# A local-attention feed-forward stage, layer by layer, is rewritten as four passes of one layer and one sequence each

## The reference, cut to what matters

```
x = x + 0.5 * L0_ffn(layernorm(x))       # local attention and GEGLU, 2 layers
x = x + L0_attn(layernorm(x))            # attention with relative positions
x = x + 0.5 * L0_ffn(layernorm(x))
x = x + 0.5 * L1_ffn(layernorm(x))       # top 8 of 64 experts, plus a shared one
x = x + L1_attn(layernorm(x))            # state space model
x = x + 0.5 * L1_ffn(layernorm(x))

def _layer(x, wqkv, qs, ksc, wo, lg, lb, w1, b1, w2, b2):   # inside L0_ffn
    h = shift_token(x)                       # second half of the features one token later
    q, k, v = split(h @ wqkv, 3)             # 8 heads of 64
    q, k = l2norm(q) * qs, l2norm(k) * ksc
    q, k = rotary_xpos(q, k)
    o = local_attention(q, k, v)             # each token sees itself and the 64 before it
    x = x + o @ wo
    h = layernorm(shift_token(x)) * lg + lb
    a, g = split(h @ w1 + b1, 2)             # 341 each
    return x + (a * gelu(g)) @ w2 + b2
```

## Time and profile before

| | us |
|---|---|
| median of 3 runs (5562.16 to 5575.62) | 5565.12 |
| the profiled execution, its own time | 5573.75 |
| its span | 5572.0 |
| a feed-forward stage with experts, from its norm to its end | 231.3 |
| the two layers of a feed-forward stage alone | 240.6 |
| an attention stage with the state space model (its two ends read off the trace) | 164 |

### The profile page before, as it was taken

How to read it: one execution, slowest core, us unless ns; L and a number is a source line. 1 busy time by engine, 2 the same in 40 slices (tenths; PEclk the granted TensorE clock), 3 DMA queues, 4 the chain that set the end, 5 groups by cost and what they waited for, 6 DMA issues and landing times. The chain is left out here.

```text
span 5572.0 us, 51193 instructions
## 1 busy us (share of the span) xinstructions
PE 4237.3 (76%) x16034; PEld 2320.4 (42%) x16034; DVE 3172.3 (57%) x5382; ACT 2506.1 (45%) x5663; POOL 1501.4 (27%) x1096
## 2 busy tenths in 40 slices
PE   5686688787876878777886878768787787877756
PEld 3444444444533544344444434434443444444312
DVE  3323365765556555755557655575556655575576
ACT  2343344543454434634446444554346444464332
POOL 2102131531125112421215322251114312252111
PEclk7787798998998989989899889989899898999877
DMA  3020011210121110311103111121112111031122
GB/s 89 1 76 0 2 47 39 83 52 28 48 65 59 44 36 31 105 35 33 43 20 106 45 31 47 59 67 48 31 36 96 40 33 44 23 106 43 37 70 69
DMA packets 188817, 273.95 MB, mean 49 GB/s; under 512 B 23448, under 2 KB 102900, under 8 KB 188532
## 3 DMA queue, kind: packets, MB, share of 16 engines
q1 hardware_dynamic: 167652, 234.89, 13.4%
q10 hardware_dynamic: 20880, 35.52, 2.1%
HBM read 215.54 MB, written 54.79 MB: 49 GB/s over the span
## 5 line engine op out<-in xcount | busy, mean ns | idle before, releaser
L638 DVE SCALAR_TENSOR_TENSOR psum<-work,psum 128x512 f32<-128x512 f32 x528 | 366.6, 694 | 600.5 <-ACT work L576 599.4
L1463 POOL MEMSET work<- 128x256 f32 x32 | 10.0, 311 | 2323.8 <-POOLq L1265 1165.4
L1426 ACT ACTIVATE work<-psum,work 128x128 f32<-128x128 f32 (+1 forms) x1024 | 389.8, 393 | 421.6 <-DVE work L1523 421.4
L553 PE MATMUL psum<-work,w_up 128*128 128x512 f32 x1024 | 572.7, 643 | 1.5 <-DVE work L632 1.5
L558 PE MATMUL psum<-work,w_down 128*128 128x512 f32 x1024 | 551.9, 621 | 20.4 <-DVE work L645 18.2
L576 ACT ACTIVATE work<-psum 128x512 f32<-128x512 f32 x528 | 317.4, 601 | 345.2 <-PE psum L553 276.3
L1288 PE MATMUL psum<-ident,work 128*128 128x128 f32 x1024 | 187.1, 343 | 330.7 <-POOL work L1477 330.6
L1344 PE MATMUL psum<-work 128*128 128x64 f32 x3072 | 415.8, 291 | 0.0
L1344 PEld LDWEIGHTS psum<-work 128*128 128x128 f32 x3072 | 388.1, 204 | 39.0 <-issue 32.2
L1470 POOL TENSOR_TENSOR work<-work,minus_half 128x16 f32<-128x16 f32 x128 | 374.3, 2924 | 10.7
L645 DVE TENSOR_TENSOR work<-work,psum 128x512 f32<-128x512 f32 x512 | 351.4, 686 | 19.6 <-DMA work<-expert_weight_rows 2.1
(11 more groups left out here) (210 smaller groups left out, 8834.6 us busy)
## 6 DMA issues: line engine op xcount, KB each, us to landing
work<-expert_weight_rows SPq DMA_DIRECT2D x1024, 128.0 KB, 2.9
position_scores<-work SPq DMA_DIRECT2D x64, 768.0 KB, 3.5
work<-position_scores SPq DMA_DIRECT2D x64, 512.0 KB, 3.8
work<-state_readout_rows ACTq DMA_DIRECT2D x72, 256.0 KB, 3.4
cent<-state_readout_rows ACTq DMA_DIRECT2D x32, 256.0 KB, 3.6
sq<-state_readout_rows ACTq DMA_DIRECT2D x24, 256.0 KB, 3.6
rows<-in_L_attn_q SPq DMA_DIRECT2D x8, 256.0 KB, 3.7
expert_weight_rows<-work SPq DMA_DIRECT2D x16, 128.0 KB, 2.3
```

The costliest lines, as they stand in the source:

```text
L553: nc.tensor.matmul(UP, b.w_up[:, p * 128:(p + 1) * 128], self.xn, start=True, stop=True).then_inc(self.up, 1)
L638: v.scalar_tensor_tensor(out=UP, in0=self.tanh_h[p % self.turns][0:rows], scalar=1.0, in1=UP, op0=ALU.add, op1=ALU.mult).then_inc(self.sil ...
L1426: ins = s.activation(prob_of(u)[:, i, first:first + n], score_banks[:, i, first:first + n], ACT.Exp, bias=neg_max[:, t, 4 * half + i:4 * h ...
```

## The change

The two layers become four passes: pass i is layer i // 2 of sequence i % 2, with 256 tokens. Each pass is cut in steps: 5 of projection (P), 8 of attention (A) and 7 of mixing, norm and gated product (M). They run in one block, in seven phases: P of pass 0; A of 0 beside P of 1; A of 1 beside M of 0; M of 1 beside P of 2; A of 2 beside P of 3; A of 3 beside M of 2; M of 3. A step k of every engine's program holds the attention step, then the projection or mixing step, then the expert steps due. Those are dealt out as 3, 5, 5, 7, 5, 5 and 8, with 2 in the norm block (step 2, the top 8, moves from there to the first phase).

PSUM is dealt anew: scores have banks 0 and 1, turned weights bank 2 alone (six groups of four turned blocks in a pass, copied by ACT and DVE in turn), values bank 3, projection banks 4 and 5 (one product in each, evicted one by one), mixing 4 and 5 or 0 and 1, so that the experts keep only bank 6 for their up products beside bank 7 for the sum. The products behind the attention have 256 columns instead of 512. Where the experts run alone (the last round) they have three banks as before.

```diff
--- before.py
+++ after.py
...
-    BESIDE = ((5, 6), 7)
+    BESIDE = ((6,), 7)
...
-        self.aff = bank(b, self.ups[1])[:, 0:TILES * EXPERTS].rearrange("p (t e) -> p t e", t=TILES)
-        self.norm_banks = self.ups[0:2]
+        self.aff = bank(b, self.sum_bank)[:, 0:TILES * EXPERTS].rearrange("p (t e) -> p t e", t=TILES)
+        self.norm_banks = (self.ups[0], self.sum_bank)
...
-            beside.tensor(pe, upto=3)
...
-    for l in range(DEPTH):
-        ffn_layer(nc, b, prefixed(f"layer{l}"), l, beside, space, transfers if l == 0 else ([], None))
+    LocalFfn(nc, b, prefixed("passes"), space).run(beside, transfers)
...
+    PASSES = DEPTH * GROUP_SEQS
+    PROJECT, ATTEND, MIX = 5, 8, 7
...
+    @staticmethod
+    def where(i):
+        return i // GROUP_SEQS, slice(i % GROUP_SEQS * SEQ, (i % GROUP_SEQS + 1) * SEQ)
...
+    def mix_banks(i):
+        return (4, 5) if i % 2 == 0 else (0, 1)
...
+    def project_tensor(self, pe, i, k):
+        nc, b = self.nc, self.b
+        l, cols = self.where(i)
+        if k == 0:
+            pe.wait_ge(self.rows_shifted, i + 1)
+        for n in (2 * k, 2 * k + 1):
+            out = bank(b, 4 + n % 2)
+            if 10 * i + n >= 2:
+                pe.wait_ge(self.evicted, 10 * i + n - 1)
+            if k < 3:
+                t, part = n // 3, n % 3
+                at = cols.start + t * 128
+                nc.tensor.matmul(out, b.xn[:, at:at + 128], b.wqkv[:, l, part * INNER:(part + 1) * INNER],
+                                 start=True, stop=True).then_inc(self.projected, 1)
+            else:
+                t, part = k - 3, n % 2
+                if part == 0:
+                    pe.wait_ge(self.rotated, 2 * i + t + 1)
+                for j in range(4):
+                    at = part * INNER + j * 128
+                    ins = nc.tensor.transpose(out[:, j * 128:(j + 1) * 128], self.cosine[t][:, at:at + 128], b.ident[:])
+                ins.then_inc(self.projected, 1)
+
+    def project_scalar(self, act, i, k):
...
+    def project_vector(self, dve, i, t):
+        v, b = self.nc.vector, self.b
+        l, tile = i // GROUP_SEQS, 2 * i + t
+        dve.wait_ge(self.squared, tile + 1)
+        if i >= 1:
+            dve.wait_ge(self.rotated, tile - 1)
+            dve.wait_ge(self.projected, 10 * (i - 1) + 8 + 2 * t)
+        v.tensor_reduce(self.lens[t], self.sine[t].rearrange("p (h d) -> p h d", d=LD), AX, ALU.add).then_inc(self.summed, 1)
+        dve.wait_ge(self.summed, tile + 1)
+        for k in (1, 0):
+            r8, c8, s8 = (x[t][:, k * INNER:(k + 1) * INNER].rearrange("p (h d) -> p h d", d=LD) for x in (self.raw, self.cosine, self.sine))
+            table = lambda n, x0, x1: b.rope_w[:, l, n, t, x0:x1].unsqueeze(1).broadcast_to([128, LH, x1 - x0])
+            v.tensor_tensor(c8, r8, table(2 * k, 0, LD), ALU.mult)
+            v.tensor_tensor(s8[:, :, 0:32], r8[:, :, 32:64], table(2 * k + 1, 0, 32), ALU.mult)
+            ins = v.tensor_tensor(s8[:, :, 32:64], r8[:, :, 0:32], table(2 * k + 1, 32, 64), ALU.mult)
+            ins.then_inc(self.split if k == 0 else self.k_split, 1)
+        dve.wait_ge(self.k_split, tile + 1)
+        keys = slice(INNER, 2 * INNER)
+        v.tensor_tensor(self.cosine[t][:, keys], self.cosine[t][:, keys], self.sine[t][:, keys], ALU.add).then_inc(self.k_added, 1)
+
...
+    def turn_probs(self, pe, i, m):
+        nc, b = self.nc, self.b
+        u = self.UNIT_OF[m]
+        pe.wait_ge(self.exped, 4 * i + u + 1)
+        self.group_copied(pe, i, m - 1)
+        for n in range(4):
+            x, c = (n, 1) if u < 2 else (2 * (m % 2) + n // 2, n % 2)
+            ins = nc.tensor.transpose(bank(b, 2)[:, n * 128:(n + 1) * 128], self.probs[u % 2][:, x, c * 128:(c + 1) * 128], b.ident[:])
+        ins.then_inc(self.p_turned, 1)
+
...
+    def attend_tensor(self, pe, i, k):
+        if k == 0:
+            self.unit_scores(pe, i, 0)
+        elif k <= self.GROUPS:
+            m = k - 1
+            self.turn_probs(pe, i, m)
+            u = self.UNIT_OF[m]
+            if m in (0, 1, 2):
+                self.unit_scores(pe, i, u + 1)
+            if m >= 1:
+                self.values(pe, i, m - 1)
+        else:
...
+    def attend_scalar(self, act, i, k):
+        if k == 0:
+            if i == 0:
+                act.wait_ge(self.zeroed, 1)
+            self.exps(act, i, 0)
+        elif k <= self.GROUPS:
+            m = k - 1
+            if m % 2 == 0:
+                self.copy_probs(act, self.nc.scalar.copy, i, m, self.p_copied_a)
+            if m in (0, 1, 2):
+                self.exps(act, i, self.UNIT_OF[m] + 1)
...
+    def attend_vector(self, dve, i, k):
+        if k == 0:
+            self.maxima(dve, i, 0)
+        elif k <= self.GROUPS:
+            m = k - 1
+            if m in (0, 1, 2):
+                self.maxima(dve, i, self.UNIT_OF[m] + 1)
+            if m % 2 == 1:
+                self.copy_probs(dve, self.nc.vector.tensor_copy, i, m, self.p_copied_v)
+            if m == 2:
+                self.scale_heads(dve, i, 0)
+        else:
...
+    def run(self, beside, transfers):
+        P, A, M = self.PROJECT, self.ATTEND, self.MIX
+        due = lambda guests, k, n: (k + 1) * guests // n - k * guests // n
+
+        with self.nc.Block() as block:
+            @block.tensor
+            def _(pe):
+                for k in range(P):
+                    self.project_tensor(pe, 0, k)
+                    if k >= 2:
+                        beside.tensor(pe)
+                for k in range(A):
+                    self.attend_tensor(pe, 0, k)
+                    if k < P:
+                        self.project_tensor(pe, 1, k)
+                    beside.tensor(pe, due(5, k, A))
+                for k in range(A):
+                    self.attend_tensor(pe, 1, k)
+                    if k < M:
+                        self.mix_tensor(pe, 0, k)
+                    beside.tensor(pe, due(5, k, A))
+                for k in range(M):
+                    if k < P:
+                        self.project_tensor(pe, 2, k)
+                    self.mix_tensor(pe, 1, k)
+                    beside.tensor(pe, due(7, k, M))
+                for k in range(A):
+                    self.attend_tensor(pe, 2, k)
+                    if k < P:
+                        self.project_tensor(pe, 3, k)
+                    beside.tensor(pe, due(5, k, A))
+                for k in range(A):
+                    self.attend_tensor(pe, 3, k)
+                    if k < M:
+                        self.mix_tensor(pe, 2, k)
+                    beside.tensor(pe, due(5, k, A))
+                for k in range(M):
+                    self.mix_tensor(pe, 3, k)
+                    beside.tensor(pe, due(8, k, M))
...
+                for i in range(GROUP_SEQS):
+                    self.shift(dve, self.where(i)[1]).then_inc(self.rows_shifted, 1)
+                for k in range(P):
+                    if k in (1, 3):
+                        self.project_vector(dve, 0, k // 2)
+                    if k >= 2:
+                        beside.vector(dve)
+                for k in range(A):
+                    self.attend_vector(dve, 0, k)
+                    if k in (1, 3):
+                        self.project_vector(dve, 1, k // 2)
...
```

634 lines of the change are left out of this document (312 added, 322 removed).

## The result

| | before | after |
|---|---|---|
| median, us | 5570.17 (4 runs) | 5665.93 (4 runs, 5664.88 to 5670.4) |
| span of the profiled execution | 5572.0 | 5668.5 |
| a steady feed-forward stage, from its norm on | 231.3 | 244.8 |
| two layers of the two stages alone | 240.5 and 240.6 | 191.8 and 200.3 |

The ratio is 1.0175, with a 95% interval of 1.0157 to 1.0192. The change is slower by 96 us. The forecast was slower by 72, at 5637 us, with a range of 5480 to 5760.

The account below looks back on a forecast made before the run. Projection phases were taken as bound by a chain through four engines, attention with experts by TensorE. Fourteen stages at +8.5 us (+119) and the stages alone at -47 gave +72 on 5565: 5637 us, range 5480 to 5760.

Parts of the forecast that it names:

- tile 1's chain: A pass's second projected tile: DVE sums, POOL's power, addition and scaling, then TensorE turns it, 7.85 us after DVE starts.
- half clock: TensorE's slow clock behind a large gap ahead of the second tile's turning: 2.5 us charged in each of three phases.
- A steady stage: One of fourteen feed-forward stages with experts: the laid-out phases sum to 239.8 us against 231.3, +8.5.
- P alone: First phase, projection of pass 0 with no attention or mixing beside it: 23 us, second tile ready at 20.9.
- M beside P: Mixing of pass 1 beside projection of pass 2: 26.6 us of TensorE, waits 5.8 and 2.0, clock 2.5, total 36.9 us.
- The stages alone: The two stages at the start without experts: 217 us against 240.6 each, -47 us for both, bounds 200 to 235.
- The gap of 2.16 us: TensorE waits for step 2's exponentials in A beside P, the row maximum standing behind DVE's tile and expert: 1.7 us.
- Rival (a): Packing wins: laid-out waits overlap and the clock stays full; a stage 219 us, the kernel 5343 us; chance 0.12.
- Rival (b): Draw to small gain: laid-out waits right, no half clock; +1 us a stage, 5532 us (5480 to 5560); chance 0.25.
- Rival (c): Single expert bank decides: +23 us a stage, 5952 us, or likelier 5 or 6 us a stage, 5715; chance 0.13.
- Rival (d): A drain comes with table loads ahead of exponentials and gelu, as the skill page says: 133 us more, 5770; chance 0.02.
- table loads: ACT's loads rise from 9 to 16 a stage, 9.1 us; only 1.3 and part of the norm's wait on the path.

Follow-up runs that it names:

- Experiments 3: Changed kernel with the turning of a pass's second projected tile one step later on TensorE and ScalarE: 5512.61 us, ratio 0.9904.
- 8: Changed kernel with the expert put ahead of the second tile's turning in the fifth step beside a projection, on TensorE and ScalarE: 5522.86 us, ratio 0.9914.
- experiment 12: Experiment 11's order on VectorE, but with the second tile's turning one step later in place of one expert's step later: 5425.94 us, ratio 0.9739.
- experiment 4: Changed kernel with four idle products of 0.86 us on TensorE ahead of the wait for the second tile: 5601.55 us, ratio 1.0057.
- experiment 2: Kernel before, with the experts beside a stage given only bank 6 for up products instead of banks 5 and 6: 5576.72 us, ratio 1.0007.
- Experiment 5: Changed kernel with an exponential and a tanh in place of the passes' logarithm and gelu, leaving out 13 of 16 table loads a stage: 5603.88 us, ratio 1.0072.
- experiment 11: Experiment 10's kernel, with the second step's expert moved behind the third step's row maximum on VectorE in A beside P: 5461.3 us, ratio 0.9796.
- experiment 10: Kernel of 8, with VectorE's fourth-step tile piece opened between keys and queries for the expert's (beside mixing, the norm's) two operations: 5587.9 us, ratio 1.0023.

## Why the prediction was right, and where it wasn't

- **The side and the mechanism** were right: a stage is bound in its projection phases by tile 1's chain through DVE and POOL, and the change adds stretches in which TensorE must wait in order for it. Experiments 3 and 8 move that one wait, by a step or by one expert, and take 153 and 143 us. The place of the half clock was right in two of the three phases only: in the first A beside P it stands ahead of tile 1's gap and not behind it, so that 38.6 predicted against 38.8 measured is in part luck.
- **A steady stage: +8.5 predicted, +13.5 measured.** The mis-sized terms are P alone (23, measured 26.0), M beside P (36.9, measured 39.5) and the norm (8, measured 9.1), 6.7 us together; the others were within 1.7 us, and sum to 1.7 us less than predicted. In P alone DVE decides. The top 8, laid out at 2.5 us (10.6 to 13.1), takes 4.16 (2657.02 to 2661.18), since its last operation is five times as long as in the kernel before. So tile 1's sum starts at 15.0 and not at 13.1, its chain to the turning takes 8.42 us and not 7.8, and 2.6 us and not 2.1 are left behind it, at half clock: 3.0 us in all. The clock of 0.63 in the window is little of it, since TensorE is idle for 11.75 us ahead of the two turnings. In M beside P I had charged 2.5 us for the clock, in one stretch; there are two, behind the gap in the norm's chain and behind tile 1's. The charge was worked out of half-clock stretches of 3.4 to 6.8 us, of which the rows of before show the 6.8 alone. These errors of 5.0 us a stage were multiplied by fourteen: +70 us.
- **The stages alone: -47 predicted, -89 measured.** 217 us was to be compared with 191.8 and 200.3. The terms that failed are the attention phases, A beside M above all. I had 36 us for each A beside M, without a layout, and they take 30.1 and 27.1 in the first stage (clock 0.89 and 1.00) and 30.8 and 30.6 in the second (0.82 twice). A beside P, taken near its half-clock value (37 and 37.5), takes 33.0 and 31.4, and 35.1 and 33.3. The whole stages have 0.86 and 0.77 where before had 0.72 and 0.70. The lower bound of 200, given for a mostly full clock, was nearer than the 217, and the first stage is below it.
- The two errors have opposite signs, so the sum (+72 against +96.5) looks better than its terms.
- **The gap of 2.16 us** at step 2 and its cause, the maximum behind tile 0's piece and the expert, were in the layout at 1.7 us. What I didn't see is that the half clock of the first stretch comes with it and not with the larger gap: that is so in the rows after, and the exchange that shortens it in 11 brings the clock to 0.98. What in that exchange the clock answers to wasn't isolated.
- **Rival (a)**, that the work packs, fell for the order as given. The best order found, experiment 12's, has 220.5 us for seven phases; with a norm block of 9.1 that is 229.6 for a stage, below the 231.3 of before, and still above the rival's 219. **Rival (b)** had the waits without the half clock. The half clock came, and even with two of its stretches filled (experiment 4) a round is 672.2 us, 8.7 a stage above before, where the rival had 1. **Rival (c)**, the single bank, fell in its strong form: 1.0007 in experiment 2 (in the old order), and 6.4 us of waits a stage at L553 in the kernel after, a little over the 6 that I had named as the most for the forecast and far from the 20 for the rival. Its weak form (5 or 6 us a stage above the layout) has the size of what was measured, but not its place: 4.1 of the 6.7 us are in P alone and the norm, where no up product waits. What those 6.4 us cost in the new order wasn't measured. **Rival (d)** fell too, see below.
- The table loads were put at 1.3 us of path a stage and part of the norm's wait. Experiment 5 has 4.4 us for thirteen of them, 2.4 by proportion for the seven that are new.

## What to carry to other kernels

Where engines work in order, ask what stands behind a wait and not only how long the awaited chain is: free work (here an expert's products) put ahead of the wait paid 143 us, with the chain as long as before. No experiment shortened the chain. Moving one filler from ahead of the wait to behind it, to relieve another engine, cost 63 us. A filler is free only if it doesn't wait itself: in the first stretch the expert put ahead waited 2.88 us for its bank, and nothing was won. Look at durations again where work moves beside another engine's: an operation of 0.42 us took 2.13 beside POOL. When a change is close, look at the short gaps that come before a long one, since two orders with the same long gaps differed by 127 us, and what else differed in their first stretch was one gap of 2.16 or 0.90 us and the clock behind it.

## What the runs showed of the hardware

VectorE's operation L618 (128x256, from `work` to `work`) took 0.42 us with POOL idle in the kernel before, and 2.13 us in the kernel after, where it started 0.06 us behind POOL's 1.90 us scaling (2659.02 and 2658.96); it is as long in each of fourteen stages.

A gap of 3.1 us on TensorE didn't cost its clock in experiment 11 (1.00 over 197.7 us, with two such gaps in it), and was followed by 10.2 us at half clock in experiment 10, where the stretch ahead of it held a gap of 2.16 us and 3.4 us at half clock. I had charged the half clock to the size of a gap; the rows don't bear that out. What exactly decides is open.

A table load takes 1.28 us and the next activation starts right behind it, in the kernel after too:

```profile
2681.24 1.28 ACT L576 ACT_TABLE_LOAD   x1
...
2682.53 0.60 ACT L576 ACTIVATE work<-psum 128x512 f32<-128x512 f32 x1
```

From one start to the other is 1.29 us. The Trainium skill, ScalarE: Activation LUTs, section "What ACT_TABLE_LOAD costs", has a drain of about the load's length behind it; this trace disagrees here as in the earlier trace rows.
